# Another order of VectorE's work in the second of four expert passes

## The chip, the cores and the metric

The kernel runs on one core of one Trainium2 chip. The metric is the device time of one execution in microseconds (us); a kernel's time is the median of its runs. Five engines work side by side and meet only at semaphores: PE (TensorE, matrix products), DVE (VectorE), ACT (ScalarE), POOL (GpSimd) and SP (SyncE, which issues the DMAs here). Each takes its own instructions in the order of its program.

## The reference

For each of 2 batch entries of 512 tokens and width 1024:

```
x = x + fake_quant(layernorm(x)) @ fake_quant(ctx)          # a quantised product
h = layernorm(x)
ratio  = mean|h[text tokens]| / mean|h[vision tokens]|      # one number per batch entry
scores = softmax([h, ratio] @ gate_w + gate_b)              # 3 experts
(v0, v1), (j0, j1) = top 2 of scores; v normalised by their sum
                     # the experts are those of the entry's first token
for i in (0, 1):                                            # a "pair": batch entry b, its expert j_i
    x = x + v_i * (act_j(h @ w1[j_i] + b1[j_i]) @ w2[j_i] + b2[j_i])
```

act_j is tanh, gelu or silu. The matrices are fp32.

## The kernel before, in words

**Pairs.** After the quantised product the kernel walks through four pairs p = 0 to 3 (p = 0 and 1 are batch entry 0, p = 2 and 3 are entry 1). A pair has a first product, h @ w1, in 8 blocks of 24 matmuls (line 1638), and a second one, act @ w2, that is done in Strassen's manner with 7 block products (list `PRODUCTS`, i = 0 to 6), each in two halves j = 0, 1 of 12 matmuls (line 1607). Every fp32 operand is split in a high and a low part (`hi`, `lo`), and each product is the sum hi·hi + hi·lo + lo·hi. ACT makes the high parts, DVE the low ones.

**Weights.** A pair has 11 weight "quarters": q + 0 to q + 3 are w1, q + 4, 5, 9 are loaded blocks of w2, and q + 8, 6, 10, 7 are the sums T3, T2, T4, T1 of such blocks, made by DVE in this order (`t3_sum`, `t2_sum`, `t4_sum`, `t1_sum`, line 1023 for the last). Each quarter is split in two chunks by `w_hi_quarter` (ACT, line 643) and then `w_lo_quarter` (DVE, line 992). Block product i of the second product reads quarter q + 4 + i: product 3 needs q + 7, which is the sum T1, and product 4 needs q + 8.

**The other DVE steps.** `late_lo` (line 1065) makes the low part of an activation block after ACT's `late_hi` (line 671). `result(p, i)` (line 1089) takes product i out of its two PSUM banks ("evicts" it), scales it by the gate and adds it into xres. Product 4 goes to the PSUM bank of product 2, so each half of product 4 waits for the same half of `result(p, 2)` (line 1662 and the wait under it).

**Entry 1's h and its router, in pair 1.** While PE works on pair 1, the h of entry 1 is made ready, 128 tokens (a tile) at a time: POOL normalises it (line 469), PE turns it with 8 transposes (`transpose_h(1, t)`, line 1433), ACT's `split_h` (line 602) and DVE's `h_lo(1, t)` (line 876) split it. Tiles 2 and 3 come in the second product: PE turns tile 2 between the halves' end of product 0 and product 1, and tile 3 after product 2, ahead of product 3. Tile 3 is turned in PSUM banks 0 and 1, where product 1 had been put, so `transpose_h(1, 3)` first waits until both halves of `result(1, 1)` are done (line 1431, `y2_done` at 2 * NP + 4). Product 3 goes to banks 2 and 3, where tile 2 was turned, and waits for `h_lo(1, 2)`, and with it for the first chunk of `w_lo_quarter(q + 7)`.
The router of entry 1 is `router_bias`, `dot_scores` and `score_steps` on DVE (lines 893 to 944, 16 small instructions), then `gate_exp` on ACT, `choose_experts` (lines 951 to 970) and `gate_values` on DVE. `choose_experts` names the expert whose w1 SP loads next (`load_w1`, line 325), which also waits for `w_lo` of earlier quarters.

**ACT's order** around this is fixed and is not touched: `w_hi_quarter(q + 6)`, `late_hi(0)`, `split_h(1, 2)`, `w_hi_quarter(q + 7)`, `late_hi(1)`, `split_h(1, 3)`, `w_hi_quarter(q + 8)`, `late_hi(2)`, `w_hi_quarter(q + 9)`, `gate_exp(1)`, `late_hi(3)`, `w_hi_quarter(q + 10)`. `w_hi_quarter(q + 7)` waits for T1 and `split_h(1, 3)` for PE's transposes of tile 3.

Of the kernel before, what the change touches and what calls it, by code (L numbers as in the profile page):

```python
# [91 lines left out]
def build(nc, x, ctx_in, s1, z1, s2, z2, gate_w, gate_b, w1, b1, w2, b2, out):  # L92
# [8 lines left out]
    with ExitStack() as st:  # L101
# [190 lines left out]
        def region(q):  # L292

            return raw[:, 2 * REGION[q]:2 * REGION[q] + 2, :].rearrange("p c (k n) -> p (c k) n", k=2)
# [483 lines left out]
        def _(dve):  # L778
            steps = [0]

            def then(ins):

                steps[0] += 1
                ins.then_inc(dve_step, 1)
                dve.wait_ge(dve_step, steps[0])
# [20 lines left out]
            def h_stats(i):  # L806

                dve.wait_ge(x1_ready, i + 1)
                tile_stats(i, xres[:, i, :], mvh, h_stats_ready)
# [61 lines left out]
            def h_lo(b, t):  # L871

                i = b * TT + t
                for c in range(2):
                    dve.wait_ge(hT_hi_ready, 2 * i + c + 1)
                    V.tensor_tensor(hT_lo[:, 4 * c:4 * c + 4, t * P:(t + 1) * P],  # L876
                                    ps[:, HT_BANK[b][t] + c, :].rearrange("p (k s) -> p k s", k=4),
                                    hT_hi[:, 4 * c:4 * c + 4, t * P:(t + 1) * P].bitcast(F32),
                                    ALU.subtract).then_inc(hT_lo_ready, 1)
# [8 lines left out]
            def router_bias(b):  # L888

                dve.wait_ge(ratio_ps, b + 1)  # L890
                if b == 0:
                    dve.wait_ge(gw_ready, 1)
                V.tensor_reduce(vts[:], ps[:, RATIO_BANK[b], 0:2 * TT].rearrange("p (a t) -> p a t", a=2),
                                AX.X, ALU.add).then_inc(ratio_read, 1)
                dve.wait_ge(ratio_read, b + 1)
                then(V.tensor_scalar(ratio[:, 0:1], vts[:, 0:1], 1.0 / (VISION * D), 1e-8, ALU.mult, ALU.add))
                then(V.reciprocal(ratio[:, 1:2], ratio[:, 0:1]))
                then(V.tensor_scalar(ratio[:, 2:3], vts[:, 1:2], 1.0 / ((S - VISION) * D), ratio[:, 1:2],
                                     ALU.mult, ALU.mult))
                then(V.scalar_tensor_tensor(out=gbias[:], in0=gw_last, scalar=ratio[:, 2:3], in1=gb,  # L900
                                            op0=ALU.mult, op1=ALU.add))
# [94 lines left out]
            def w_lo_quarter(n):  # L996

                for c in range(2):
                    w_lo_chunk(n, c)
# [19 lines left out]
            def t1_sum(p):  # L1019

                dve.wait_ge(t_ready, 4 * p + 3)
                dve.wait_ge(w_lo_ready, 2 * (QUARTERS * p + 6) + 2)
                V.tensor_tensor(region(7), region(9), region(6), ALU.subtract).then_inc(t_ready, 1)  # L1023
# [37 lines left out]
            def late_lo(p, j):  # L1061

                slot, f, c = ((0, 0, 2 * P), (1, 0, 0), (0, TT, 0), (2, TT, 2 * P))[j]
                dve.wait_ge(late_hi_ready, 4 * p + j + 1)
                V.tensor_tensor(a_lo[slot][:], act_f[:, f:f + TT, c:c + 2 * P], a_hi[slot][:].bitcast(F32),
                                ALU.subtract).then_inc(late_lo_ready, 1)
# [10 lines left out]
            def result(p, i):  # L1077

                _, bank, _, first, half = PRODUCTS[i]
                for j in range(2):  # L1080
                    n = 2 * NP * p + 2 * i + j
                    if i == 0:
                        dve.wait_ge(b2_used, TT * p + TT)
                    elif i in (1, 4, 5):
                        dve.wait_ge(y2_done, n + 1 - 2 * {1: 1, 4: 1, 5: 3}[i])
                    dve.wait_ge(g2_done, n + 1)
                    t = first + j
                    xt = xres[:, p // TOP_K * TT + t, half * H:(half + 1) * H]
                    V.scalar_tensor_tensor(out=xt, in0=ps[:, bank + j, :], scalar=gate[:, p * TT + t:p * TT + t + 1],  # L1089
                                           in1=xt, op0=ALU.mult, op1=ALU.add).then_inc(y2_done, 1)  # L1090
# [119 lines left out]
            for p in range(PAIRS):  # L1210
                q = QUARTERS * p
                if p == 1:
                    gate_dot(3)
                    gate_dot(4)
                for f in range(KT):
                    k = f - TT
                    dve.wait_ge(act_ready, p * KT + f + 1)
                    a_lo_block(p, f)
                    if f < TT:
                        s3_sum(p, f)  # L1220
                    else:
                        s1_sum(p, k)
                        if k:
                            s1_lo(p, k - 1)
                            s2_sum(p, k - 1)
                            s4_sum(p, k - 1)
                    if f == 0:
                        if p > 0:
                            w_lo_quarter(q + 3)
                        else:  # L1230
                            pass
                    elif f == 1:
                        if p > 0:
                            t3_sum(p)
                        else:
                            pass
                    elif f == 2 and p == 0:
                        w_lo_quarter(2)
                        w_lo_quarter(3)
                    if f < TT:  # L1240
                        bias_add(p, f)
                    if p == 0 and f == 0:
                        h_stats(5)
                        h_stats(6)
                    elif p == 0 and f == 1:
                        h_stats(7)
                        gate_dot(0)
                    elif p == 0 and f == 2:
                        gate_dot(1)
                        gate_dot(2)  # L1250
                    elif p == 1 and f in (0, 1):
                        gate_dot(5 + f)
                    elif p == 1 and f == 2:
                        gate_dot(7)
                        gate_dot(8)
                    elif p == 1 and f in (3, 4, 5):
                        gate_dot(6 + f)
                    if f == 3:
                        w_lo_quarter(q + 4)
                        if p > 0:  # L1260
                            t2_sum(p)
                    elif f == 4:
                        w_lo_quarter(q + 5)
                        if p > 0:
                            t4_sum(p)
                        else:
                            t3_sum(p)
                    elif f == 5 and p == 0:
                        t2_sum(p)
                    elif f == 6 and p == 0:  # L1270
                        t4_sum(p)
                    if p == 1 and f == TT:
                        tokens_abs(1)
                if p == 1:
                    h_lo(1, 0)
                    h_lo(1, 1)
                s1_lo(p, 3)
                s2_sum(p, 3)
                s4_sum(p, 3)
                w_lo_quarter(q + 6)  # L1280
                late_lo(p, 0)
                result(p, 0)
                if p == 1:
                    h_lo(1, 2)
                t1_sum(p)
                result(p, 1)
                if p == 1:
                    router_bias(1)
                    dot_scores()
                    score_steps()  # L1290
                w_lo_quarter(q + 7)
                late_lo(p, 1)
                if p == 1:
                    h_lo(1, 3)
                w_lo_quarter(q + 8)
                result(p, 2)
                late_lo(p, 2)
                result(p, 3)
                w_lo_quarter(q + 9)
                if p == 1:  # L1300
                    choose_experts(1)
                result(p, 4)
                late_lo(p, 3)
                w_lo_quarter(q + 10)
                result(p, 5)
                if p + 1 < PAIRS:
                    w_lo_quarter(q + QUARTERS)
                    w_lo_quarter(q + QUARTERS + 1)
                result(p, 6)
                if p == 1:  # L1310
                    gate_values(1)
                if p + 1 < PAIRS:
                    w_lo_quarter(q + QUARTERS + 2)
# [380 lines left out]
```

## Time and profile before

| | us |
|---|---|
| median of 3 runs (lowest to highest) | 404.01 (403.53 to 404.82) |
| the profiled execution | 403.35 |
| its span in the profile | 401.5 |
| PE busy | 384.8 (96%) |
| DVE busy | 347.2 (86%) |
| ACT busy | 195.2 (49%) |

A row of a timeline gives the start in us from the span's start, the time, the engine, the source line, the operation with output<-inputs, and the count of instructions merged in it. In brackets stands how long the engine had been idle before it and what ended that. The time of a row with several instructions runs from the first start to the last end. An instruction's start can lie before the end of the one ahead of it on the same engine, since they are pipelined: what it costs in a queue is the distance to the next start.

### The profile page before, as it was taken

What the parts mean: (1) busy time and instruction counts of PE and PEld (TensorE: products, weight loads), DVE (VectorE), ACT (ScalarE), POOL (GpSimd) and SP (SyncE); (2) the same over time, 40 slices, a digit from 0 to 9 for tenths busy, and PEclk for the clock granted to TensorE, in tenths of its full rate; (3) what the DMA queues carried; (4) which work ended last, traced back from release to release, by engine and by line L of the source; (5) the groups of instructions that cost most, each with busy time, mean ns of one, the idle gap of its engine ahead of it and who ended that gap; (6) DMA issues with size and microseconds to landing.
All of it is one profiled execution on the core that took longest, in us unless ns stands there. A gap on an engine that the chain in (4) does not pass through costs nothing.

```text
span 401.5 us, 5230 instructions
## 1 busy us (share of the span) xinstructions
PE 384.8 (96%) x1860; PEld 303.4 (76%) x1860; DVE 347.2 (86%) x539; ACT 195.2 (49%) x253; POOL 53.6 (13%) x70
## 2 busy tenths in 40 slices
PE   1999999999999999999989999999999999999996
PEld 1435737888888888888867888888888888888885
DVE  8799869999999799999999997694997865949973
ACT  3568645174447625651846263343476333424720
POOL 8648400530000000063100000000000000000000
PEclk9999999999999999999998999999999999999999
DMA  8996049441006585000000499400055880000112
GB/s 316 411 408 282 2 137 376 169 148 61 2 0 205 177 299 211 2 0 2 0 0 2 147 379 385 189 0 2 0 176 192 241 283 2 0 0 2 53 52 106
DMA packets 23981, 54.39 MB, mean 135 GB/s; under 512 B 1776, under 2 KB 1808, under 8 KB 23824
## 3 DMA queue, kind: packets, MB, share of 16 engines
q1 hardware_dynamic: 23888, 54.01, 37.5%
q8 instruction: 15, 0.25, 0.3%
q14 instruction: 14, 0.11, 0.1%
q10 hardware_dynamic: 64, 0.02, 0.0%
HBM read 49.83 MB, written 4.19 MB: 135 GB/s over the span
## 4 chain that ended last, share of the span: by engine, by line
PE 84%; DVE 9%; ACT 2%; issue 2%; DMA 1%; ACTq 1%; POOL 0%; DVEq 0%; POOLq 0%
PE ps L1638 43%; PE ps L1607 34%; PE ps L1401 4%; DVE xres L867 2%; DVE hT_lo L876 1%; DMA b1n<-in_L_ffn_b_dram 1%; DVE bn L796 1%; DVE xres L1089 1%; PE ps L1433 1%; DVE w_lo L992 1%; PE ps L1389 1%; DVE raw L1023 1%; PE ps L1333 0%; DVE q L830 0%; DVE act_f L1058 0%
## 5 line engine op out<-in xcount | busy, mean ns | idle before, releaser
L643 ACT ACTIVATE w_hi<-raw 128x1024 fp32r<-128x1024 f32 x88 | 88.5, 1053 | 45.6 <-DVE raw L1023 22.6
L992 DVE TENSOR_TENSOR w_lo<-raw,w_hi 128x1024 fp32r<-128x1024 f32 x88 | 103.6, 1219 | 0.6
L1638 PE MATMUL ps<-hT_hi,w_hi 128*128 128x512 f32 x256 | 99.9, 390 | 0.0
L1638 PE MATMUL ps<-hT_hi,w_lo 128*128 128x512 f32 x256 | 99.6, 389 | 0.0
L1638 PE MATMUL ps<-hT_lo,w_hi 128*128 128x512 f32 x256 | 99.6, 389 | 0.0
L1607 PE MATMUL ps<-w_hi,a_hi 128*128 128x512 f32 x224 | 88.2, 394 | 2.6 <-DVE w_lo L992 2.5
L1607 PE MATMUL ps<-w_lo,a_hi 128*128 128x512 f32 x224 | 87.7, 391 | 0.0
L1607 PE MATMUL ps<-w_hi,a_lo 128*128 128x512 f32 x224 | 87.6, 391 | 0.0
L731 ACT ACTIVATE act_f<-ps,b1T 128x512 f32<-128x512 f32 x32 | 22.1, 690 | 109.1 <-PE ps L1638 109.0
L1638 PEld LDWEIGHTS ps<-hT_hi,w_hi 128*128 128x128 f32 x256 | 48.1, 188 | 10.2 <-issue 0.2
L1638 PEld LDWEIGHTS ps<-hT_hi,w_lo 128*128 128x128 f32 x256 | 48.1, 188 | 10.0
L1638 PEld LDWEIGHTS ps<-hT_lo,w_hi 128*128 128x128 f32 x256 | 48.1, 188 | 9.8
L1607 PEld LDWEIGHTS ps<-w_hi,a_hi 128*128 128x128 f32 x224 | 42.4, 189 | 12.1 <-issue 3.2
L1089 DVE SCALAR_TENSOR_TENSOR xres<-ps,gate,xres 128x512 f32<-128x512 f32 x56 | 40.1, 744 | 11.7 <-PE ps L1607 11.7
L1607 PEld LDWEIGHTS ps<-w_lo,a_hi 128*128 128x128 f32 x224 | 42.5, 190 | 8.8
L1607 PEld LDWEIGHTS ps<-w_hi,a_lo 128*128 128x128 f32 x224 | 42.4, 189 | 8.9
L1027 DVE TENSOR_TENSOR a_lo<-act_f,a_hi 128x256 fp32r<-128x256 f32 x32 | 13.4, 419 | 24.8 <-ACT a_hi L737 24.7
L1401 PE MATMUL ps<-ctxq,q1T 128*128 128x512 f16 x128 | 31.4, 386 | 1.7 <-DVE xres L867 1.1
L469 POOL TENSOR_SCALAR b2row<-xres,h_rstd,h_shift 128x1024 f32<-128x1024 f32 x4 | 11.6, 2900 | 102.2 <-DVE xres L1074 86.6
L1401 PEld LDWEIGHTS ps<-ctxq,q1T 128*128 128x128 f16 x128 | 11.4, 98 | 17.4 <-issue 5.4
L671 ACT ACTIVATE a_hi<-act_f 128x1024 fp32r<-128x1024 f32 x16 | 16.9, 1058 | 12.1 <-PE ps L1607 12.1
L1074 DVE SCALAR_TENSOR_TENSOR xres<-b2row,gate,xres 128x1024 f32<-128x1024 f32 x16 | 20.5, 1279 | 0.0
(156 smaller groups left out, 369.7 us busy)
## 6 DMA issues: line engine op xcount, KB each, us to landing
raw<-in_L_ffn_w_dram SPq DMA_DIRECT2D x64, 512.0 KB, 5.6
raw<-in_ctx_dram SPq DMA_DIRECT2D x16, 512.0 KB, 11.5
xres<-in_x_dram SPq DMA_DIRECT2D x8, 512.0 KB, 9.5
out_dram<-xres SPq DMA_DIRECT2D x16, 256.0 KB, 4.2
b2row<-in_L_ffn_b_dram SPq DMA_DIRECT2D x4, 512.0 KB, 6.8
gate_rows<-in_L_ffn_gate_w_dram SPq DMA_DIRECT2D x1, 1536.0 KB, 18.3
small<-in_L_xattn_x_scale_dram ACTq DMA_DIRECT2D x2, 0.0 KB
small<-in_L_xattn_x_zp_dram ACTq DMA_DIRECT2D x2, 0.0 KB
```

Of the source, the lines that this page charges most:

```text
L469: G.tensor_scalar(b2row[:], xres[:, i, :], h_rstd[:, i:i + 1], h_shift[:, i:i + 1], ALU.mult, ALU.add).then_inc(h_ready["pool"], 1)
L643: nc.scalar.activation(w_hi[n % SLOTS][:, 2 * c:2 * c + 2, :], region(q)[:, 2 * c:2 * c + 2, :], ACT.Copy).then_inc(w_hi_ready, 1)
L671: nc.scalar.activation(dst[:], src, ACT.Copy).then_inc(late_hi_ready, 1)
L731: nc.scalar.activation(act_f[:, f, :], ps[:, G1_BANK + f % 2, :], EXPERT_ACT[ee], bias=bias)
L867: last = V.scalar_tensor_tensor(out=xt, in0=ps[:, ATT_BANK[b][t] + c, :], scalar=s12, in1=xt, op0=ALU.mult, op1=ALU.add)
L992: V.tensor_tensor(w_lo[n % SLOTS][:, 2 * c:2 * c + 2, :], region(n % QUARTERS)[:, 2 * c:2 * c + 2, :], w_hi[n % SLOTS][:, 2 * c:2 * c + 2, ...
L1027: V.tensor_tensor(a_lo[f // TT][:, f % TT, :], act_f[:, f, 0:2 * P], a_hi[f // TT][:, f % TT, :].bitcast(F32), ALU.subtract).then_inc(a_lo ...
L1074: V.scalar_tensor_tensor(out=xt, in0=b2row[:], scalar=gate[:, p * TT + t:p * TT + t + 1], in1=xt, op0=ALU.mult, op1=ALU.add).then_inc(b2_u ...
L1089: V.scalar_tensor_tensor(out=xt, in0=ps[:, bank + j, :], scalar=gate[:, p * TT + t:p * TT + t + 1], in1=xt, op0=ALU.mult, op1=ALU.add).the ...
L1401: T.matmul(ps[:, ATT_BANK[b][t] + c, :], q1T[b][:, k, t * P:(t + 1) * P], ctxq[b][:, k, c * H:(c + 1) * H], start=k == 0, stop=False)
L1607: last = T.matmul(ps[:, bank + j, :], a[slot][:, k, tok], v[w][:, k, :], start=fresh and n == 0, stop=n == 3 * TT - 1, skip_group_check=True)
L1638: last = T.matmul(ps[:, G1_BANK + f % 2, :], w[q % SLOTS][:, k % TT, fs], h[:, k, :], start=n == 0, stop=n == 3 * KT - 1)
```

## The change

Only the order of DVE's steps in pair 1 is changed; for the other three pairs the list stays as it was. Before, in pair 1, after `result(1, 0)`: `h_lo(1, 2)`, `t1_sum`, `result(1, 1)`, router, `w_lo` q + 7, `late_lo(1)`, `h_lo(1, 3)`, `w_lo` q + 8, `result(1, 2)`. After: `t1_sum`, `h_lo(1, 2)`, `w_lo` q + 7, `result(1, 1)`, `late_lo(1)`, `w_lo` q + 8, `h_lo(1, 3)`, router, `result(1, 2)`.

```diff
@@ -1280,19 +1280,21 @@
                 w_lo_quarter(q + 6)
                 late_lo(p, 0)
                 result(p, 0)
+                t1_sum(p)
                 if p == 1:
                     h_lo(1, 2)
-                t1_sum(p)
-                result(p, 1)
+                else:
+                    result(p, 1)
+                w_lo_quarter(q + 7)
                 if p == 1:
+                    result(p, 1)
+                late_lo(p, 1)
+                w_lo_quarter(q + 8)
+                if p == 1:
+                    h_lo(1, 3)
                     router_bias(1)
                     dot_scores()
                     score_steps()
-                w_lo_quarter(q + 7)
-                late_lo(p, 1)
-                if p == 1:
-                    h_lo(1, 3)
-                w_lo_quarter(q + 8)
                 result(p, 2)
                 late_lo(p, 2)
                 result(p, 3)
```

## Rows read from the trace of the kernel before

**Rows 1.** The page, its share of the chain that ended last, by engine.
```profile
PE 84%; DVE 9%; ACT 2%; issue 2%; DMA 1%; ACTq 1%; POOL 0%; DVEq 0%; POOLq 0%
```

**Rows 2.** Waits of PE (who waited for whom: us in total, times, longest).
```profile
PE ps L1607 <- DVE w_lo L992: 2.5, 1, 2.5
```

**Rows 3.** Chain that ended last, in order of time (start, us, what).
```profile
210.22 1.15 DVE w_lo L992
211.37 0.14 issue
211.50 23.53 PE ps L1607 x96
235.03 43.52 PE ps L1638 x192
```

**Rows 4.** Timeline of PE from the end of product 2 to pair 2.
```profile
207.71 0.39 PE L1607 MATMUL ps<-w_hi,a_lo 128*128 128x512 f32 x1
207.94 1.03 PE L1433 MATMUL ps<-ident,b2row 128*128 128x128 f32 x8
211.50 0.77 PE L1607 MATMUL ps<-w_hi,a_hi 128*128 128x512 f32 x1 [2.52 <-DVE w_lo L992]
...
218.55 0.39 PE L1607 MATMUL ps<-w_hi,a_hi 128*128 128x512 f32 x1
...
234.87 0.39 PE L1638 MATMUL ps<-hT_hi,w_hi 128*128 128x512 f32 x1
```

**Rows 5.** PE by stretches: stretch, length, PE busy (x instructions), granted clock, DMA share, GB/s.
```profile
208.00:209.00 1.00, 0.98 (x9) 1.00 0.00 0
...
212.00:213.00 1.00, 1.00 (x4) 0.50 0.00 0
...
215.00:216.00 1.00, 1.00 (x6) 1.00 0.00 0
```

**Rows 6.** Timeline of DVE in the second product of pair 1.
```profile
201.53 1.40 DVE L1089 SCALAR_TENSOR_TENSOR xres<-ps,gate,xres 128x512 f32<-128x512 f32 x2
202.85 1.27 DVE L876 TENSOR_TENSOR hT_lo<-ps,hT_hi 128x512 fp32r<-128x512 f32 x2
204.05 2.27 DVE L1023 TENSOR_TENSOR raw<-raw 128x2048 f32<-128x2048 f32 x1
206.25 1.40 DVE L1089 SCALAR_TENSOR_TENSOR xres<-ps,gate,xres 128x512 f32<-128x512 f32 x2
207.57 0.15 DVE L893 TENSOR_REDUCE vts<-ps 128x2 f32<-128x8 f32 x1
...
210.14 2.35 DVE L992 TENSOR_TENSOR w_lo<-raw,w_hi 128x1024 fp32r<-128x1024 f32 x2
212.41 1.22 DVE L1065 TENSOR_TENSOR a_lo<-act_f,a_hi 128x1024 fp32r<-128x1024 f32 x1
213.54 1.28 DVE L876 TENSOR_TENSOR hT_lo<-ps,hT_hi 128x512 fp32r<-128x512 f32 x2
...
217.01 1.40 DVE L1089 SCALAR_TENSOR_TENSOR xres<-ps,gate,xres 128x512 f32<-128x512 f32 x2
...
223.05 0.15 DVE L951 TENSOR_TENSOR sel<-ex 128x4 f32<-128x4 f32 x1
```

**Rows 7.** Timeline of ACT in the same stretch.
```profile
206.42 2.01 ACT L643 ACTIVATE w_hi<-raw 128x1024 fp32r<-128x1024 f32 x2 [7.28 <-DVE raw L1023]
208.33 1.04 ACT L671 ACTIVATE a_hi<-act_f 128x1024 fp32r<-128x1024 f32 x1
209.27 1.06 ACT L602 ACTIVATE hT_hi<-ps 128x512 fp32r<-128x512 f32 x2
210.23 2.00 ACT L643 ACTIVATE w_hi<-raw 128x1024 fp32r<-128x1024 f32 x2
...
228.72 1.06 ACT L643 ACTIVATE w_hi<-raw 128x1024 fp32r<-128x1024 f32 x1 [7.01 <-DMA raw<-in_L_ffn_w_dram]
```

**Rows 8.** Timeline of SP's DMA issues: the first weights of pair 2.
```profile
224.87 2.33 SPq L325 DMA_DIRECT2D raw<-in_L_ffn_w_dram  x4
```

## The prediction

> **What bounds the kernel now.** I read the page's chain first: PE carries 84% of what ended last and DVE 9% [rows 1]. In PE's waits one row concerns the stretch of the change: 2.5 us, once, for a w_lo [rows 2]. The chain in order of time places it: the router on DVE, then a w_lo of 1.15 us, 0.14 us of signalling, PE at 211.50, and from there PE alone (four further rows of PE follow the two that stand there) up to the last eviction [rows 3]. So whatever moves PE's start of the later products moves the end one for one, unless something later has slack to give back, and there is no PE wait later to shrink. PE's timeline shows the hole: product 2 ends at about 208.1, 8 transposes of tile 3 run 207.94 to 208.97, and product 3 starts 2.52 us later [rows 4]. It then runs at the lower clock: granted 1.00 before the hole, 0.50 at 212 (2.4 and 1.2 GHz), 1.00 again at 215 [rows 5]. The full pace is (234.87 − 218.55) / 72 = 0.227 us per matmul, so the 24 matmuls of a product take 5.44 us; product 3 took 218.55 − 211.50 = 7.05 [rows 4]. The lower clock cost 1.61 us of that, and the hole as a whole about 4.1 us.
>
> **The change part by part.** Nothing is added or removed; the steps keep their durations. As queue costs I take distances between starts [rows 6]: result 206.25 to 207.57 = 1.32, its last end 1.40 after its start; h_lo 202.85 to 204.05 = 1.20; t1_sum 2.20; router 207.57 to 210.14 = 2.57; w_lo quarter 210.14 to 212.41 = 2.27; late_lo 1.13. Result 0 still starts at 201.53, so the first moved step starts at 202.85.
>
> *T1 ahead of tile 2's h_lo.* t1_sum runs 202.85 to 205.05, 1.20 earlier. ACT's w_hi of q + 7 started 2.37 after t1_sum's start [rows 6, 7], so now at 205.22; its two instructions take 2.01 together and start 0.95 apart (1.91 to the next over two), so its first chunk is done at about 206.28. DVE does h_lo(1, 2) from 205.05 to 206.25 meanwhile, and w_lo q + 7 from 206.30 to 208.57, with its first chunk done at 207.5. Product 3 has its w_lo and its tile 2 before product 2 ends at 207.94. That wait is gone: the old hole's cause is repaired.
>
> *Result 1 behind w_lo q + 7.* It starts at 208.57 and not 206.25, and ends at 209.97. Who waits for it is PE: transpose_h(1, 3) is ahead of product 3 in PE's order and wants both halves of result(1, 1) out of banks 0 and 1. Before, that was done at 207.65, under the end of product 2. Now PE stands idle from 208.10 to 209.97 + 0.14 [the signalling of rows 3] = 210.11: a new hole of 2.0 us. The transposes then take 0.87 (modelled end 211.14), product 3 starts at 210.98, half a microsecond before its old start. If the clock falls as before, 3.2 us after the last real matmul of product 2 (that is about 211.3), product 3 takes 7.05 and ends at 218.0; if not, it ends at 216.4.
>
> *What hangs on the transposes.* ACT's split_h(1, 3) waits for them and starts at about 211.17. Queued behind it on ACT is w_hi q + 8, which used to start at 210.23 [rows 7]; now at 211.17 + 0.96 = 212.13, first chunk done at 213.19. DVE has finished result 1 at 209.89 and late_lo(1) at 211.02 and, since w_lo q + 8 is next in its queue, stands still until 213.21, about 2.2 us. Then w_lo q + 8 to 215.48, h_lo(1, 3) to 216.68, the router to 219.25, and result 2 only then: first half done 0.75 later at 220.00 (before: start 217.01, end about 217.75, 0.8 us ahead of product 4). Product 4's first half writes product 2's bank and can't start before 220.00 + 0.14 = 220.14. It started at 218.55 [rows 4]. That is **+1.59 us**, whichever way product 3 went.
>
> *The clock once more.* PE is idle from product 3's end (218.0, or 216.4) to 220.14: 2.2 us, or 3.7. The row we have is a hole of 2.52 us of idleness with 0.9 us of transposes ahead of it, after which 1.61 us was lost at 1.2 GHz [rows 4, 5]. A second such fall costs between 0 and 1.6; below nothing isn't possible, since product 4 can't go faster than the full pace. I take the row's own price rounded down a little for a shorter hole, 1.55, as the hole plus the tail of the slow product 3 before it resembles it most. Sum: 1.59 + 1.55 = **+3.1 us**.
>
> *The transposes themselves.* They took 1.03 at full clock. At the lower clock they take at most twice that, and then everything from split_h on is later by up to 0.9 us. I take nothing, because the fall came 3.2 us after the last matmul and they end 2.9 after it; 0.9 stays as the upper end. The Trainium skill (TensorE: Matmul & The Clock Gate, Part 4: PE-mode transpose) gives about 390 ns for one in isolation and 275 ns in a kernel's context. By the first figure the transposes after the hole would begin 0.12 us slower, which would make an estimate of +3.2 us.
>
> *Behind product 4.* Result 2 starts 2.24 later than before (219.25 against 217.01), so late_lo(2), result 3, w_lo q + 9 and choose_experts (223.05 [rows 6]) move by 2.24: SP's issue of pair 2's w1 from 224.87 to 227.1 [rows 8], ACT's first w_hi of them from 228.72 to 231.0 [rows 7]. PE enters pair 2 at 234.87 + 3.1 = 238.0. Even with result 5 and four w_lo chunks behind it the first chunk is there by about 235 and the last by 238.6, needed 18 matmuls (4.1 us) into the block. So nothing there adds to the sum; if the second fall of the clock doesn't come, PE enters at 236.5 and about 2 us of cover is left. gate_exp on ACT now waits for the router's end at 219.25 and late_hi(3) behind it ends at about 220.5, long before product 6 needs it. No queue of POOL or SP is passed otherwise.
>
> The sum is made against the profiled execution: span 401.5 + 3.1, with its 1.85 around the span 406.5, against 403.35. That execution lies 0.66 under the median of the runs shown, so on the median's scale 404.01 + 3.1 = 407.1 us.
>
> **The rivals.**
> (a) Forecast: new hole at the transposes, longer hole ahead of product 4, two falls of the clock. +3.1.
> (b) Same chain, but the second hole (2.2 us, shorter than the 2.52 of the row) leaves the clock at 2.4 GHz: +1.6, 405.6 us. Against it: PE will have had two holes within 12 us. For it: the shorter idleness, with matmuls on both sides and no transposes.
> (c) The transposes run at the lower clock too, so the chain through split_h is 0.9 longer: 3.1 + 0.9 = +4.0, 408.0.
> (d) The other side: T1's early start wins and nothing takes its place, because w_hi q + 8 isn't held up behind split_h(1, 3). DVE would go on at 211.02 with w_lo q + 8 to 213.29, h_lo to 214.49, router to 217.06, result 2's first half at 217.81, product 4 free at 217.95, just when a product 3 slowed by the clock ends (217.97). That is 218.55 − 217.97 = −0.6, 403.4 us. It decides at result 2's start: before about 217.7 the change loses nothing, after it every microsecond counts. For it speaks only that ACT has time to spare; against it, that a_hi at 208.33 had its inputs when product 1 was done (before 202.5, as product 2's 5.44 us end at 207.94) and still ran behind the w_hi that waited until 206.42 [rows 7]. ACT doesn't pass a waiting instruction by. The Trainium skill says the same as a rule (PSUM — Partial Sum Buffer, Engine vs sequencer instructions): the queues of ScalarE and VectorE are strict FIFO. By that rule (d) is out; with a queue that could reorder the estimate would be its −0.6.
> (e) The change does less than it says: I mis-size the ACT to DVE handoffs or the pace of the small router steps by 1 us and the clock falls once only. +0.6, within the noise.
>
> **How the numbers follow.** (a) 0.55, (b) 0.25, (c) 0.08, (d) 0.04, (e) 0.08. The likeliest gives 407.1 us. The range takes in (a), (b) with 0.6 us of scatter below (the runs shown lie 0.5 under and 0.8 over their median), and (c) with little above: 405.0 to 408.4. It leaves out (d) and part of (e). What a measurement of this kernel can tell from no change is about 0.3%, 1.2 us. (a) and (c) are slower; of (b), at +1.6, I give a fifth to "same"; (d) and (e) are mostly "same", with little left for faster: slower 0.84, same 0.13, faster 0.03.
>
> **What would show it.** In the changed kernel's PE waits, the old row for w_lo before product 3 is gone and two new ones stand there: one of about 2.0 us before line 1433, ended by DVE's xres at line 1089, and one of 2.2 to 3.7 us before line 1607, ended by the same line. DVE shows an idle of about 2.2 us ended by ACT's w_hi, ACT's split_h starts at about 211.2, and the granted clock is 0.50 in two stretches, near 212 and 221. Product 4 starts at 220.1. PE runs without a wait from there. I am wrong if transpose_h(1, 3) starts before 209, or if product 4 starts without a wait for result 2.

## Result and the profile after

The changed kernel takes 407.40 us (median of 3 runs, 407.24 to 407.97) against 404.01: a ratio of 1.0085, 95% interval 1.0054 to 1.0115. It is slower by 3.4 us; 407.1 was predicted, in a range of 405.0 to 408.4. The profiled execution took 407.4, with a span of 405.7.

Lines of the kernel after are 2 higher than before: 1433 is now 1435 (transposes of h), 1607 is 1609 (second product), 1638 is 1640 (first product). First the waits of PE: who waited for whom, us in total, times, longest.

```profile
PE ps L1435 <- DVE xres L1089: 2.0, 1, 2.0
PE ps L1609 <- issue: 1.9, 1, 1.9
```

The row of [rows 2] is gone, and these two are new. The second is put down to "issue", but its place tells what it waited for: it ends at 220.97, 0.09 us after the first half of result 2 has ended (it starts at 220.13, below, and one half of an eviction takes 0.75 us, as in the last row of the chain). The step that product 4 waits for by the program is just that half. The chain that ended last, in order of time (start, us, what):

```profile
209.45 1.33 DVE xres L1089 x2
210.78 0.14 issue
210.91 1.07 PE ps L1435 x8
211.98 7.07 PE ps L1609 x24
219.05 1.92 issue
220.97 18.21 PE ps L1609 x72
239.18 43.52 PE ps L1640 x192
...
402.42 0.75 DVE xres L1089
```

Against [rows 3] the chain now goes over the eviction (xres, line 1089) and the transposes to product 3, and has a second hole ahead of product 4. Every moment here is 0.77 us later than on the old trace for a reason outside the change. I read that off the chain's row where pair 0's first product begins, 63.08 before and 63.85 after:

```profile
63.85 43.75 PE ps L1640 x192
```

So I count each kernel's **stage length** in its profiled execution, from that row to the same row of pair 2: 235.03 − 63.08 = 171.95 before and 239.18 − 63.85 = 175.33 after, **+3.38 us**, where the prediction had +3.1. VectorE and ScalarE in between (timelines; start, us, in brackets idle time ahead and what ended it):

```profile
203.63 2.27 DVE L1023 TENSOR_TENSOR raw<-raw 128x2048 f32<-128x2048 f32 x1
205.82 1.27 DVE L876 TENSOR_TENSOR hT_lo<-ps,hT_hi 128x512 fp32r<-128x512 f32 x2
207.09 2.36 DVE L992 TENSOR_TENSOR w_lo<-raw,w_hi 128x1024 fp32r<-128x1024 f32 x2
209.36 1.40 DVE L1089 SCALAR_TENSOR_TENSOR xres<-ps,gate,xres 128x512 f32<-128x512 f32 x2
...
214.08 2.36 DVE L992 TENSOR_TENSOR w_lo<-raw,w_hi 128x1024 fp32r<-128x1024 f32 x2 [2.18 <-ACT w_hi L643]
216.36 1.28 DVE L876 TENSOR_TENSOR hT_lo<-ps,hT_hi 128x512 fp32r<-128x512 f32 x2
217.56 0.15 DVE L893 TENSOR_REDUCE vts<-ps 128x2 f32<-128x8 f32 x1
...
220.13 1.40 DVE L1089 SCALAR_TENSOR_TENSOR xres<-ps,gate,xres 128x512 f32<-128x512 f32 x2
```

```profile
205.99 2.01 ACT L643 ACTIVATE w_hi<-raw 128x1024 fp32r<-128x1024 f32 x2 [6.09 <-DVE raw L1023]
207.91 1.04 ACT L671 ACTIVATE a_hi<-act_f 128x1024 fp32r<-128x1024 f32 x1
212.01 1.08 ACT L602 ACTIVATE hT_hi<-ps 128x512 fp32r<-128x512 f32 x2 [3.07 <-PE ps L1435]
212.99 2.00 ACT L643 ACTIVATE w_hi<-raw 128x1024 fp32r<-128x1024 f32 x2
```

The w_lo of q + 7 moved from 210.14 [rows 6] to 207.09, in time for product 3. Result 1 moved from 206.25 to 209.36, and PE stood before the transposes for it. ScalarE's split of tile 3 (line 602) could only start when the transposes were done, 3.07 us after its queue had come to it; w_hi q + 8 behind it moved from 210.23 [rows 7] to 212.99, and VectorE stood still for 2.18 us ahead of w_lo q + 8. PE by stretches:

```profile
209.00:210.00 1.00, 0.00 (x0) 1.00 0.00 0
...
213.00:214.00 1.00, 1.00 (x4) 0.50 0.00 0
...
219.00:220.00 1.00, 0.05 (x1) 1.00 0.00 0
...
223.00:224.00 1.00, 1.00 (x4) 0.50 0.00 0
```

The columns are the stretch, its length, PE's busy share with the number of matmuls, the granted clock as a share of 2.4 GHz, the DMA share and GB/s. There are two holes and two stretches at 1.2 GHz, where [rows 5] had one.

### The profile page after: what moved, and what is told of

It is laid out like the page before. It is cut to its first block, busy times and chain, and to the rows that moved or that the text cites. A ratio compares the mean times of both kernels' runs of the same rounds, so it can differ in the third digit from the quotient of the medians.

```text
span 405.7 us, 5230 instructions
## 1 busy us (share of the span) xinstructions
PE 386.7 (95%) x1860; PEld 304.6 (75%) x1860; DVE 346.3 (85%) x539; ACT 195.3 (48%) x253; POOL 53.5 (13%) x70
## 4 chain that ended last, share of the span: by engine, by line
PE 83%; DVE 9%; DMA 2%; issue 2%; ACT 2%; SPq 1%; POOL 1%; DVEq 0%; POOLq 0%; ACTq 0%
PE ps L1640 43%; PE ps L1609 34%; PE ps L1403 3%; DMA raw<-in_ctx_dram 2%; DVE xres L867 2%; DVE hT_lo L876 1%; DVE bn L796 1%; PE ps L1435 1%; DVE xres L1089 1%; DVE w_lo L992 1%; PE ps L1391 1%; DVE raw L1023 1%; DVE q L830 0%; SPq L314 0%; SPq L319 0%
## 5 line engine op out<-in xcount | busy, mean ns | idle before, releaser
L1609 PE MATMUL ps<-w_hi,a_lo 128*128 128x512 f32 x224 | 88.5, 395 | 0.0
```

The source lines that it names most:

```text
L1609: last = T.matmul(ps[:, bank + j, :], a[slot][:, k, tok], v[w][:, k, :], start=fresh and n == 0, stop=n == 3 * TT - 1, skip_group_check=True)
```

## The experiments

All were timed in 5 rounds beside the kernel before on the same chip. A time behind "against" is that kernel's, and an interval is one of 95%. A stage length is that of one execution, the profiled one, so what the clock did in that execution is in it. The diffs are cut down to pair 1's list on VectorE. Lines in these kernels are 14 higher than before (1621 is the second product, 1447 the transposes, 1652 the first product) where the kernel has a list of its own for pair 1.

### undo_evict: result 1 back ahead of w_lo q + 7

```diff
 t1_sum(p)
 h_lo(1, 2)
+result(p, 1)
 w_lo_quarter(q + 7)
-result(p, 1)
 late_lo(p, 1)
```

> The changed kernel with one part undone: result(1, 1) stands ahead of w_lo q + 7 again (T1, h tile 2, result 1, w_lo q + 7, late_lo 1, w_lo q + 8, h tile 3, router, result 2). My theory: the changed kernel loses 2.0 us ahead of the transposes because they wait for result 1. Here result 1 ends at 207.65 on the old trace's scale, so PE has no wait ahead of the transposes, product 3 starts at about 208.9 (changed: 211.0), and result 2, still behind the router, ends its first half at 217.84, so product 4 starts at 218.0 after a hole of 3.7 us and the clock falls there for 1.6 us. Product 6 starts 1.0 later than before: 405.0 us, between before (404.0) and the changed kernel (407.4). Rival, in which only the router's place costs anything and the eviction's place nothing: 407.4, as the changed kernel. Rival, in which the second fall of the clock is no part of the price: 403.4.

Measured: 404.69 us against 403.94; ratio 1.0031 (1.0015 to 1.0046). Stage length 173.05, **+1.10** over the one of before; +1.0 was expected. Chain:

```profile
208.84 5.71 PE ps L1621 x24
214.54 3.30 issue
217.84 18.19 PE ps L1621 x72
```

The hole ahead of the transposes is gone and product 3 starts at 208.84 at full clock. VectorE has no standstill ahead of w_lo q + 8 either. The later hole remains, at 3.30 us longer than the changed kernel's, as product 3 ends sooner. So product 4 is held by result 2 behind the router even with result 1 in its old place. Undoing the eviction's move takes away 2.28 of the 3.38 us.

### undo_router: the router behind result 2

```diff
 w_lo_quarter(q + 8)
 h_lo(1, 3)
+result(p, 2)
 router_bias(1)
 dot_scores()
 score_steps()
-result(p, 2)
```

> The changed kernel with only the router moved behind result(1, 2): T1, h tile 2, w_lo q + 7, result 1, late_lo 1, w_lo q + 8, h tile 3, result 2, router. My theory: the hole of 2.0 us ahead of the transposes and the slow product 3 stay; result 2 comes 2.57 earlier, so product 4 starts right when product 3 ends (218.0 on the old scale) with no hole and no second fall of the clock. VectorE's list is now late later on: w_lo q + 9 about 0.9 us late for product 5, w_lo q + 10 about 0.75 more for product 6, so product 6 starts about 1.1 later than before: 405.1 us. Rival, in which the second hole comes from the transposes and not from the router's place: 407.4. Rival, in which VectorE has slack after product 4: 403.5.

Measured: 405.44 against 403.94; 1.0036 (1.0022 to 1.0050). Stage length 237.36 − 63.99 = 173.37, **+1.42**. PE's timeline, the rows with idle time ahead:

```profile
211.05 1.07 PE L1447 MATMUL ps<-ident,b2row 128*128 128x128 f32 x8 [2.05 <-DVE xres L1089]
218.54 0.47 PE L1621 MATMUL ps<-w_hi,a_hi 128*128 128x512 f32 x1 [0.93 <-issue]
225.41 0.47 PE L1621 MATMUL ps<-w_hi,a_hi 128*128 128x512 f32 x1 [1.17 <-DVE w_lo L992]
231.65 0.47 PE L1621 MATMUL ps<-w_hi,a_hi 128*128 128x512 f32 x1 [0.52 <-DVE w_lo L992]
```

The hole of 2.05 us stays and the one ahead of product 4 shrinks. Holes ahead of products 5 and 6 have come in, both ended by w_lo: VectorE is late with the sum of its work. Both rivals are out: the router's place does cost something (the first said 407.4), and there is no slack behind product 4 (the second said 403.5). Undoing the router's move takes away 1.96 us, so the two undone parts together would make 4.24, more than the whole 3.38. The two overlap, and undo_evict's profiled execution has a fall of the clock where undo_router's has none (1.00 in every microsecond from 209 to 233); how much of the surplus is which isn't shown. The hole of 0.93 instead of the expected none is there because the clock didn't fall here and product 3 ended sooner.

### t1_only: the T1 sum's place alone

```diff
 result(p, 0)
-h_lo(1, 2)
 t1_sum(p)
+h_lo(1, 2)
 result(p, 1)
```

> The kernel before with one swap alone: t1_sum ahead of h_lo(1, 2), everything else as before. ScalarE's w_hi of q + 7 starts 1.2 us earlier, but VectorE's w_lo of q + 7 is still behind the router in its queue and starts at 210.14. My theory: no change, 404.0 within 0.5, hole of 2.5 us ahead of product 3 as before. Rival, in which the T1 chain over ScalarE sets the hole: up to 1.2 us faster, 402.8.

Measured: 404.17 against 403.94; 1.0003 (0.9989 to 1.0018): no change, as expected. The early sum is worth nothing while w_lo q + 7 is queued behind the router. The rival (up to 1.2 us faster) is out. Its trace shows something I had not expected, the same hole as before and no slow stretch after it:

```profile
212.35 0.47 PE L1621 MATMUL ps<-w_hi,a_hi 128*128 128x512 f32 x1 [2.54 <-DVE w_lo L992]
218.70 0.47 PE L1621 MATMUL ps<-w_hi,a_hi 128*128 128x512 f32 x1 [0.65 <-issue]
```

```profile
213.00:214.00 1.00, 1.00 (x6) 1.00 0.00 0
```

Six matmuls in that microsecond and not four. What full clock gave back was partly lost at once: product 4 now waits 0.65 us. The stage length is 171.37, 0.58 less than in the profiled execution of before. That isn't a property of the swap. The record gives the mean granted clock of every run; one slow stretch like that of [rows 5] makes it 0.996, as in the profiled execution of before. It is 1.000 in 11 of the 50 runs of the kernel before that were timed beside the experiments and 0.994 to 0.996 in the other 39, and 1.000 in 4 of the 12 runs of t1_only. In all 8 runs of the changed kernel, after_again with them, it is 0.992 to 0.995, so the clock fell somewhere in every one.

### after_fill: keeping the array busy through the holes

```diff
 (product 2, second half)
+keep_busy(3, 8)      # 8 matmuls 128x512 into an idle PSUM bank, read by nobody
 transpose_h(1, 3)
 (product 3)
+keep_busy(4, 16)     # 16 of them, ahead of the wait for result(1, 2)
 (product 4, first half)
```

> The changed kernel plus matmuls whose output nobody reads (128x512, into an idle PSUM bank): 8 of them ahead of the transposes of tile 3 and 16 ahead of product 4, so that the array works through both holes. They take 1.8 and 3.6 us, about what the holes would last with a product 3 at full clock. My theory: VectorE's chain isn't touched, product 4 starts at 220.1 on the old scale as without them, but the clock stays at 2.4 GHz, so the second slow stretch of 1.6 to 1.7 us is gone and the first was hidden anyway: 405.7 us. Rival, in which the lower clock is not caused by the idleness or costs nothing: 407.4 or more. If the fill overruns, it costs up to 0.5.

Measured: 406.37 against 403.94; 1.0068 (1.0054 to 1.0082). Stage length 237.72 − 63.99 = 173.73, **+1.78**, against +3.38 without the fill: 1.60 us less, about what one slow stretch costs. (This diff is TensorE's list in short. Lines: 1634 is the fill, 1662 the first product.)

```profile
211.05 1.07 PE ps L1447 x8
212.12 5.47 PE ps L1621 x24
217.58 3.63 PE ps L1634 x16
221.21 16.51 PE ps L1621 x72
237.72 43.52 PE ps L1662 x192
```

The 72 matmuls of products 4 to 6 take 16.51 us here and 18.21 in the changed kernel. Product 4 starts 157.22 us behind pair 0's first product, against 157.12 in the changed kernel (221.21 − 63.99 and 220.97 − 63.85), so VectorE's chain is the same and the gain is the clock's. The granted clock is 1.00 in every microsecond from 208 to 228. By times alone the gain isn't shown. The median lies 2.43 us over the kernel before, where the expected 405.7 meant +1.7, and the ratios of the two kernels, each against the kernel before on its own chip, have intervals that overlap (1.0085 and 1.0068; after_again's 1.0098, too).

### after_again: the changed kernel once more

> The changed kernel once more, unaltered, so that it is timed on the same chip and in the same hour as the kernels beside it. All theories: about 3.4 us over the kernel before, 407.4. Whether the clock falls once or twice may differ from its first profile: a kernel with the same 2.54 us hole as the one before (only the swap of T1 and an h tile) kept 2.4 GHz throughout in its profiled execution. With one fall less the profiled execution would be 1.6 us shorter than 407.2.

Measured: 408.92 against 404.44; 1.0098 (1.0077 to 1.0119). The loss is confirmed and here larger, +4.5 us, and 408.92 lies over the upper end of the predicted range (408.4). The profiled execution, at 410.39 the longest of its runs, started pair 0 at 66.00, 2.9 us late for reasons ahead of this stage, and has a stage length of 242.17 − 66.00 = 176.17, +4.22:

```profile
214.12 5.49 PE ps L1609 x24
219.61 3.51 issue
223.12 19.05 PE ps L1609 x72
242.17 43.52 PE ps L1640 x192
```

The clock kept 2.4 GHz through product 3 (5.49 against 7.07), which gained nothing: the hole behind it grew from 1.92 to 3.51, and product 4 starts 223.12 − 66.00 = 157.12 us behind pair 0's first product, as in the first execution. Products 4 to 6 took 19.05 us, 2.5 more than at full clock. By stretches of one microsecond the clock was down before product 4 began and for longer:

```profile
222.00:223.00 1.00, 0.00 (x0) 0.50 0.00 0
...
227.00:228.00 1.00, 1.00 (x4) 0.50 0.00 0
```

The expected "one fall less is 1.6 shorter" was wrong; the slow stretch of product 3 lies in the shadow of VectorE's chain and only the one of product 4 counts.

### before_fill: the same fill in the kernel before

```diff
 transpose_h(1, 3)
+keep_busy(3, 10)
 (product 3, first half)
```

> The kernel before plus 10 matmuls that nobody reads (2.27 us of work), put between the transposes of tile 3 and product 3, in its 2.52 us hole. My theory: the hole's length is set by VectorE and stays, product 3 starts at 211.5 at full clock and would end at 216.9, but product 4 now meets result 2 at 217.9, so only 0.65 us of the 1.61 us of slow clock comes back: 403.4 against 404.0, and even less if the runs of the kernel before often keep the clock by themselves. Rival, in which the slow clock is worth its full price: 402.4.

Measured: 404.12 against 404.44; 0.9994 (0.9978 to 1.0009): no difference that can be told, and the interval takes in the expected −0.6 us. The rival (402.4, the slow stretch worth its full price) is out. The stage length is 236.15 − 64.76 = 171.39, 0.56 under that of before. The slow stretch's full price is not there to be had, since product 4 then waits 0.67 us for result 2. Part of the kernel before's runs have no fall anyway, as said under t1_only, and in those there is nothing to gain.

### evict_only: the eviction's place, on the kernel before

The early T1 sum goes with it, which t1_only showed to be worth nothing.

```diff
-h_lo(1, 2)
 t1_sum(p)
+h_lo(1, 2)
-result(p, 1)
 router_bias(1)
 dot_scores()
 score_steps()
 w_lo_quarter(q + 7)
+result(p, 1)
 late_lo(p, 1)
```

> The kernel before with T1 ahead of h tile 2 (shown to be worth nothing) and result(1, 1) behind w_lo q + 7; router and tile 3 stay where the kernel before has them: T1, h tile 2, router, w_lo q + 7, result 1, late_lo 1, h tile 3, w_lo q + 8, result 2. My theory: the transposes of tile 3 wait for result 1, now until 212.6 on the old scale, a hole of 4.5 us after product 2, a fall of the clock, product 3 from 213.5 to 220.5, result 2 done in its shadow, product 4 without a hole. Product 6 starts about 2.0 later than before: 406.0 us (0.5 to 2.8 over, by how much of product 3 is slow). Rival, in which the eviction's place costs only when the router is behind it too: 404.0.

Measured: 406.16 against 404.48; 1.0043 (1.0030 to 1.0057). Stage length 237.44 − 63.58 = 173.86, **+1.91**; 2.0 expected.

```profile
213.14 1.94 PE L1447 MATMUL ps<-ident,b2row 128*128 128x128 f32 x8 [4.54 <-DVE xres L1089]
```

The wait for result 1 ahead of the transposes does it, with no router between result 1 and result 2: the rival (404.0) is out. The hole is longer than in the changed kernel because the router stands ahead of result 1 here. The transposes themselves ran at the lower clock (1.94 us and not 1.03). With undo_evict (the router's place without the eviction's, +1.10) the two parts make 3.01 of the 3.38 us.

### w_router_early and w_router_mid: what the experiments pointed to

Three lessons together: result 1 stays ahead of w_lo q + 7, the result that PE waits for comes ahead of the w_lo behind it, and tile 3's low part, which only pair 2 needs, goes behind the second product's last w_lo.

```diff
 result(p, 0)
-h_lo(1, 2)
 t1_sum(p)
+h_lo(1, 2)
 result(p, 1)
+w_lo_quarter(q + 7)
 router_bias(1)
 dot_scores()
 score_steps()
-w_lo_quarter(q + 7)
 late_lo(p, 1)
-h_lo(1, 3)
-w_lo_quarter(q + 8)
 result(p, 2)
+w_lo_quarter(q + 8)
 late_lo(p, 2)
 result(p, 3)
 w_lo_quarter(q + 9)
 choose_experts(1)
 result(p, 4)
 late_lo(p, 3)
 w_lo_quarter(q + 10)
+h_lo(1, 3)
 result(p, 5)
```

> A new order on VectorE, ScalarE and TensorE untouched: T1, h tile 2, result 1, w_lo q + 7, router, late_lo 1, result 2, w_lo q + 8, late_lo 2, result 3, w_lo q + 9, choose_experts, result 4, late_lo 3, w_lo q + 10, h tile 3, result 5. Result 1 stays ahead of w_lo q + 7 (the transposes need it), the router fills the time in which VectorE would wait for w_hi q + 8, result 2 comes ahead of w_lo q + 8, and tile 3's low part goes behind the second product's last w_lo. My theory, on the old trace's scale: product 3 at 208.9, product 4 at 216.15 after a hole of 1.8 us, product 6 at 227.1 (VectorE's work up to the first chunk of w_lo q + 10), against 229.4 before: 401.7 us. Rival, in which any hole of 1.8 us costs another slow stretch: 402.5. Rival, in which pair 2's weights become the bound: no gain.

Measured: **401.90** against 404.44; 0.9936 (0.9918 to 0.9953), better than both kernels. One hole is left, and no fall of the clock:

```profile
216.97 0.47 PE L1621 MATMUL ps<-w_hi,a_hi 128*128 128x512 f32 x1 [1.61 <-DVE w_lo L992]
```

Stage length 233.65 − 63.77 = 169.88, **−2.07** (−2.3 expected). In w_router_mid the three router steps stand behind `late_lo(p, 2)`:

> As w_router_early but with the router behind late_lo 2: the order is T1, h tile 2, result 1, w_lo q + 7, late_lo 1, result 2, w_lo q + 8, late_lo 2, router, result 3, w_lo q + 9, choose_experts and so on. My theory: no hole ahead of product 3 or 4, one of 1.1 us ahead of product 5 and one of 0.8 us ahead of product 6, so no fall of the clock; product 6 at 227.1, since VectorE's sum of work up to it is the same: 401.7 us, the same as the early router. If the router's place alone decided, the two would differ by up to 1.8 us.

Measured: 402.77 against 404.44; 0.9955 (0.9941 to 0.9969). Stage length 234.80 − 64.93 = 169.87.

```profile
222.83 0.47 PE L1621 MATMUL ps<-w_hi,a_hi 128*128 128x512 f32 x1 [0.89 <-DVE w_lo L992]
229.07 0.47 PE L1621 MATMUL ps<-w_hi,a_hi 128*128 128x512 f32 x1 [0.54 <-DVE w_lo L992]
```

Other holes, the same stage length to 0.01 us, one execution each. In both VectorE's first chunk of w_lo q + 10 ends about 0.15 us ahead of product 6. The 1.15 us between the two profiled executions (401.95 and 403.1) are not from this stage: the second one was 1.16 late already when pair 0 began. Whether the 0.9 us between the two medians come from there too isn't shown; the intervals overlap.

### early_h3: tile 3's low part ahead again

```diff
 choose_experts(1)
+h_lo(1, 3)
 result(p, 4)
 late_lo(p, 3)
 w_lo_quarter(q + 10)
-h_lo(1, 3)
```

> w_router_early with one step moved: h tile 3 stands behind choose_experts, ahead of result 4, late_lo 3 and w_lo q + 10, and not behind them. My theory: VectorE's sum of work up to the first chunk of w_lo q + 10 sets the start of product 6, so the 1.20 us of h tile 3 comes back in full: 403.1 us if w_router_early gives 401.9. Rival, in which product 6 has slack on VectorE: 401.9.

Measured: 403.32 against 404.48; 0.9965 (0.9952 to 0.9978). Stage length 235.41 − 64.41 = 171.00, 1.12 more than in w_router_early, where 1.20 was expected. By the medians, each against its own chip's kernel before, it is 1.4 us. The rival (no loss) is out: up to product 6 it is VectorE's sum of work that counts, and h tile 3 was 1.1 us of it.

## Why the prediction was right, step by step

**T1 and w_lo q + 7.** Right. The old hole ahead of product 3 lost its cause: w_lo started at 207.09 − 0.77 = 206.32 on the old scale (predicted 206.30). By itself the early sum is worth nothing (t1_only), as w_lo q + 7 stayed behind the router there.

**Result 1 and the transposes.** Right: a hole of 2.05 us (2.0), ended by result 1, and in evict_only 4.54 (4.5) when result 1 came later still. Putting it back took away about two thirds of the loss of the stage (3.38 to 1.10, undo_evict), although only 2.05 us of idleness stood there. The rest is read off the timelines, not from an experiment that leaves it out: the hole triggers a chain. The split of tile 3, w_hi q + 8, w_lo q + 8 and result 2 were all late in turn. VectorE's standstill of 2.18 us (2.2) is in the changed kernel and not in undo_evict.

**Result 2 behind the router.** Right: product 4 started at 220.97 − 0.77 = 220.20 on the old scale (220.14), +1.65 against 218.55 [rows 4] where +1.59 was predicted.

**The clock.** The fall at product 4 stood in cases (a) and (c) with 0.63 together, and it came in both profiled executions of the changed kernel. Its price was 18.21 − 16.51 = 1.70 us by the full-clock length in after_fill (predicted 1.55), and 2.5 in the other one. So the bound "between 0 and 1.6" was too low, and that the sum of 1.65 + 1.70 = 3.35 came so near the measured 3.38 holds for the first profiled execution; in the second the same product 4 start and the dearer fall make 4.22. That the median fell 0.3 us from the forecast is in part luck for that reason. What I had not seen is that the fall in the kernel before is no fixed part of it: with the same hole t1_only kept full clock, and then waited 0.65 us for result 2. The price of the old hole's slow stretch, 1.61 us by my reading of [rows 4, 5], was therefore a gross one, and about 0.6 of it is what could be had (t1_only and before_fill, −0.58 and −0.56). That left the sum unharmed, since product 4's start is set by VectorE in the new order and the loss is counted against a profiled execution that had the fall, as 39 of 50 runs of the kernel before have. Against an execution without it the loss of the stage would have been about 0.6 us more.

**The transposes.** They were taken at full clock, and ran so: 8 took 1.07 us behind the hole against 1.03 [rows 4]. The reason given, that the fall comes 3.2 us after the last matmul and they end before it, rested on one execution (and by the prediction's own numbers they end 211.14 − 208.10 = 3.0 after it, not 2.9). It did not hold as a rule. From the end of the last 128x512 matmul ahead of a hole to the fall, read in stretches of 0.1 us, it was 3.2 us in the kernel before and 3.2 and 3.3 in the changed one, but 1.9 in after_again, 3.7 in undo_evict and 4.2 in evict_only, so the full clock at the transposes was in part luck. The first figure of the Trainium skill (TensorE: Matmul & The Clock Gate, Part 4: PE-mode transpose), about 390 ns for one in bf16 in isolation, would have made that 0.12 more; the trace shows 0.04, and a median of 273 ns for one fp32 transpose behind the hole, near the second figure, 275 ns.

**Behind product 4.** Right that nothing adds: no wait of PE follows. Pair 2's first weights moved by 2.35 us on the old scale with result 2 (2.24 predicted) and stayed covered.

**The other side.** ScalarE did not pass its waiting split: its idle time of 3.07 us stands ahead of line 602, and w_hi q + 8 starts right behind it. What w_hi q + 8 waits for itself, product 0 and the T3 sum, had been done long before. Rival (d) is refuted by that row and by the start of result 2, 219.36 on the old scale where (d) needed it before about 217.7.

## What to carry to other kernels

Before an eviction is moved down a queue, look up who else waits for its PSUM bank. Here not the next product but 8 transposes for a later pair did, and their wait held up a second engine and came back to the first. When PE's holes come from one engine's queue, add up that engine's work before each deadline of PE. Here that sum told the gain of each new order within 0.3 us of stage length: two orders with different holes had the same one to 0.01 us, and what helped was to take work without a near deadline out of the sum. A slow-clock stretch costs only what the next wait of PE does not take up: all of it behind the last wait (1.7 and 2.5 us), about 0.6 of 1.6 us in the kernel before, and nothing ahead of product 4 in the new order. So a hole is priced by what follows it.

## What the runs showed of the hardware

- Whether the granted clock fell after a hole differed between executions with the same hole: after 2.52 us it fell to 0.50 (the kernel before), after 2.54 with the same work around it, it did not (t1_only). After 2.05 us it fell in one of three profiled executions (the changed kernel; not after_again, undo_router), and after 1.92 (behind an earlier fall), 3.30, 3.51 and 4.54 each time; no profiled execution shows a fall after a hole of 1.61 us or less in this stage.
- A slow stretch lengthened the matmuls it fell on by 1.6 to 1.7 us four times (product 3 in the kernel before and in the changed one, product 4 there and in undo_evict) and by 2.5 us once (after_again). Matmuls that nobody reads, put in the hole, kept the clock at 1.00.
- The transposes follow the clock: 8 of them took 1.03 to 1.07 us at full clock and 1.94 at half.
